# Fixed experts for the first eight pairs of tiles, early weights, and identity transposes where TensorE waits, in a six-stage decoder kernel

## The reference

```python
x = _layernorm(x + _L0_attn_ref(x, ...))      # 16 heads of 128, causal, rotary
x = _layernorm(x + _L0_xattn_ref(x, ctx, ...)) # 32 heads of 16, against the context
x = _layernorm(x + _L0_ffn_ref(x, ...))       # 32 routed experts (4 of them each token, capacity 80) and a shared one
x = _layernorm(x + _L1_attn_ref(x, ...))      # 16 heads of 32, along the other axis
x = _layernorm(x + _L1_xattn_ref(x, ctx, ...)) # 16 heads of 128, RMS norm on q and k
x = _layernorm(x + _L1_ffn_ref(x, ...))
return x
```

```python
router_logits = x_flat @ gate_w.T                    # 8 experts
top_w, sel = jax.lax.top_k(router_logits, TOPK)      # TOPK = 2
top_w = jax.nn.softmax(top_w, axis=-1)
tw = jnp.zeros((n, E), dtype=x.dtype).at[tok_ids, sel].add(top_w)
g = jnp.einsum('nd,efd->enf', x_flat, gate_proj)     # F_DIM = 352
u = jnp.einsum('nd,efd->enf', x_flat, up_proj)
h = jax.nn.silu(g) * u
eo = jnp.einsum('enf,edf->end', h, down_proj)
out = jnp.einsum('end,ne->nd', eo, tw)
```

## Time and profile before

| | us |
|---|---|
| median of 3 runs | 3399.54 (3391.4 to 3400.45) |
| the profiled execution | 3412.12 |
| its span, first to last instruction | 3410.3 |
| PE busy in it | 3095.0 (91%) |
| DVE busy | 2215.1 (65%) |
| POOL busy | 1565.7 (46%) |
| ACT busy | 1446.3 (42%) |
| mean granted clock of PE | 0.957 |

### The profile page before, as it was taken

One profiled execution on the slowest core, in us unless ns is written; L12 is line 12 of the kernel. 1 busy time (PEld: TensorE's weight loads), 2 busy tenths in 40 slices (PEclk: granted clock), 3 DMA queues, 4 the chain that ended last, 5 costly groups with the idle time before them and its releaser, 6 DMA issues. The chain is left out here.

```text
span 3410.3 us, 57006 instructions
## 1 busy us (share of the span) xinstructions
PE 3095.0 (91%) x20208; PEld 2562.7 (75%) x20208; DVE 2215.1 (65%) x3877; ACT 1446.3 (42%) x3497; POOL 1565.7 (46%) x1466
## 2 busy tenths in 40 slices
PE   7999999999969999888897999699999999969992
PEld 5887878878857777665575777488888888759991
DVE  5667566567645677649775777556667677745555
ACT  3343333333336666528743333244444444324441
POOL 4544343344422343335573222355555556545555
PEclk9999999999979999889998999799999999979996
DMA  4001016022310111049612112311101001146765
GB/s 176 16 12 59 0 36 237 0 79 104 116 73 22 48 38 58 17 164 350 216 42 91 41 41 61 118 41 35 36 12 48 11 24 41 45 177 235 245 229 160
DMA packets 133264, 303.09 MB, mean 89 GB/s; under 512 B 21152, under 2 KB 33184, under 8 KB 126832
## 3 DMA queue, kind: packets, MB, share of 16 engines
q1 hardware_dynamic: 115584, 274.61, 23.6%
q0 software_dynamic: 15360, 22.16, 2.1%
q10 hardware_dynamic: 2160, 4.21, 0.4%
HBM read 231.07 MB, written 98.04 MB: 97 GB/s over the span
## 5 line engine op out<-in xcount | busy, mean ns | idle before, releaser
L398 POOL TENSOR_TENSOR a_sq<-a_tq,a_sinq 128x256 f32<-128x256 f32 x128 | 150.5, 1195 | 356.9 <-DVE a_tq L476 355.6
L364 ACT COPY a_probT<-bank 128x512 f32<-128x512 f32 x64 | 37.5, 586 | 329.1 <-PE bank L715 329.1
L398 POOL TENSOR_TENSOR a_sk<-a_tk,a_sink 128x256 f32<-128x256 f32 x128 | 123.8, 987 | 90.0 <-DVE a_tk L476 90.0
L411 POOL TENSOR_TENSOR e_sk<-e_tk 128x512 f32<-128x512 f32 x64 | 66.5, 1039 | 204.2 <-DVE e_tk L503 204.2
L348 ACT ACTIVATE a_sm<-a_sm,a_nmax 128x128 f32<-128x128 f32 x256 | 99.8, 391 | 122.6 <-DVE a_nmax L572 122.6
L353 ACT ACTIVATE e_prob<-bank,e_nb,e_rq 128x128 f32<-128x128 f32 x256 | 113.7, 454 | 86.4 <-DVE e_nb L577 86.4
L1048 POOL TENSOR_TENSOR d_prob<-d_prob,d_nmax 128x1024 f32<-128x1024 f32 x32 | 63.9, 1998 | 182.2 <-DVE d_nmax L1147 182.2
L954 ACT ACTIVATE b_prob<-bank,b_nb 128x128 f32<-128x128 f32 x512 | 139.1, 386 | 13.5 <-DVE b_nb L1152 13.2
L2334 POOL TENSOR_TENSOR m_down_lo<-cw_down,m_down_hi 128x1024 fp32r<-128x1024 f32 x32 | 93.2, 2912 | 106.4 <-ACT m_down_hi L2296 106.4
L2570 POOL TENSOR_TENSOR n_wu_lo<-nw_wu,n_wu_hi 128x1408 fp32r<-128x1408 f32 x23 | 74.3, 3232 | 128.0 <-DVE n_wu_hi L2614 128.0
L498 DVE TENSOR_TENSOR a_kr<-a_kr,a_sk 128x512 f32<-128x512 f32 x64 | 66.5, 1038 | 88.9 <-POOL a_sk L398 88.9
(11 more groups left out here) (562 smaller groups left out, 11126.9 us busy)
## 6 DMA issues: line engine op xcount, KB each, us to landing
packed<-all_zero SPq DMA_DIRECT2D x32, 1024.0 KB, 7.0
cw_up<-in_c_wgu SPq DMA_DIRECT2D x32, 1024.0 KB, 9.1
cw_down<-in_c_wd SPq DMA_DIRECT2D x32, 512.0 KB, 9.3
nw_wg<-in_f_wg SPq DMA_DIRECT2D x23, 704.0 KB, 5.9
nw_wu<-in_f_wu SPq DMA_DIRECT2D x23, 704.0 KB
nw_wd<-in_f_wd SPq DMA_DIRECT2D x23, 512.0 KB, 7.5
nw_xe<-packed SPq DMA_DIRECT2D x46, 256.0 KB, 2.7
result<-n_ye SPq DMA_DIRECT2D x46, 256.0 KB, 2.0
```

The source lines that it names most:

```text
L364: nc.scalar.copy(probT[:], pP[:, :]).then_inc(act_pt, 1)
L398: step = nc.gpsimd.tensor_tensor(o, i, s, ALU.mult)
```

## The change

Two things. First, a helper `keep_busy` issues n transposes of the identity into a bank that nobody reads, with no semaphore. It is put into PE's stream before and after `turn_x(0)` at the start of a, b, m, d, e and n, in the last unit of a and e (30 before the wait for the probabilities, 24 before the last output), and ahead of the last outputs of b and d. Nine matmuls on zeros are put in the first block.

Second, stages r and n: the first eight of the 23 pairs of tiles are now always expert 0 to 7's own first pair, so their expert and tile are known when the program is built, and only the pairs beyond come from the tables. SP loads the weights of pair 0 at once, waits for the sends, then issues the tiles of pairs 0 and 1, then the weights of pair 1. Two of r's ten sends move into the last unit of e, ahead of POOL's drain. DVE gets twelve more small operations: each expert's first pair and the rest now lie apart.

```diff
+def keep_busy(nc, bank, tile, n):
+    for _ in range(n):
+        nc.tensor.transpose(bank[:, 0:P], tile[:, 0:P], tile[:, 0:P])
...
                 if router and last:
+                    for n in (2, 3):
+                        router.send(pool, (b - 5) // 2, n)
                     pool.drain()
...
                 if r is not None and not last:
                     route(r)
+                if last:
+                    keep_busy(nc, pQ, ident, 30)
                 pe.wait_ge(v_p, done(u))
...
+            keep_busy(nc, pO, ident, busy[0])
             turn_x(0)
+            keep_busy(nc, pO, ident, busy[1])
             pe.wait_ge(g_lo, done(0))
...
             probs_v(u, 1)
+            keep_busy(nc, pQ, ident, 24)
             output(G - 1, B - 1)
...
+            keep_busy(nc, pP, ident, busy[0])
             turn_x(0)
+            keep_busy(nc, pP, ident, busy[1])
             pe.wait_ge(w_lo["q"], 1)
...
             each_batch(pe, slot)
+            keep_busy(nc, pJ, ident, busy[2])
             for e in plan["pe"][0]:
...
+            keep_busy(nc, pJ, ident, busy[3])
             output(B - 1, (0, 3 * C), False)
...
         def _(sp):
-            sp.wait_ge(tabled, 2)
+            weights.load(sp, weights.number(sp, 0, 0), 0)
+            sp.wait_ge(router.sent, 16 * K * B)
             for w in range(2):
-                weights.load(sp, weights.number(sp, 0, w), w)
-                if w == 0:
-                    sp.wait_ge(router.sent, 16 * K * B)
                 weights.load_x(sp, ..., weights.place(sp, 0, w), w)
+            weights.load(sp, weights.number(sp, 0, 1), 1)
...
         def _(pool):
-            for n in (2, 3):
-                router.send(pool, LAST - 2, n)
...
+            step(vec.tensor_scalar(first[:], first[:], float(NE), None, ALU.add))
...
+            step(vec.tensor_scalar(tsum[:], tsum[:], float(1 - NE), 0.0, ALU.add, ALU.max))
...
+            for each_expert, out in ((edge, pos), (low, own), (more, over)):
+                step(vec.tensor_tensor(prod[:], hot[:], each_expert[:]..., ALU.mult))
+                step(vec.tensor_reduce(out[:].rearrange("p b k -> p k b"), prod[:], AX.X, ALU.add))
+            step(vec.tensor_tensor(pos[:], rowf[:], pos[:], ALU.is_ge))
+            step(vec.tensor_tensor(over[:], over[:], pos[:], ALU.mult))
+            step(vec.tensor_tensor(own[:], own[:], over[:], ALU.add))
+            step(vec.tensor_tensor(rows[:], rowf[:], own[:], ALU.add))
...
+            keep_busy(nc, pO[1], ident, 12)
             turn_x(0)
+            keep_busy(nc, pO[1], ident, 6)
...
     def number(self, sp, i, w):
+        if isinstance(i, int) and 2 * i + w < self.NE:
+            return 2 * i + w
         return sp.value_load(self.expert[0:1, bass.ds(2 * i + w, 1)], ...)
...
-            with sp.Fori(0, ROUNDS - 1) as i:
+            FIXED = weights.NE // 2 - 1
+            for i in range(FIXED):
+                for w in range(2):
+                    refill(i, w)
+            with sp.Fori(FIXED, ROUNDS - 1) as i:
...
             turn_x(0, 0)
+            keep_busy(nc, pO[1], ident, 10)
             in_turns(pe, slot, ROUNDS, R, REST)
...
+                for _ in range(9):
+                    nc.tensor.matmul(psum[7][:, 0:P], zero[:, 0:P], zero[:, 0:P], start=True, stop=True)
```

More of the change, by code:

```diff
@@ L83, in split_product, with wide_attention @@
     return nc.tensor.matmul(ps, a_hi, b_hi, start=False, stop=stop)
-def wide_attention(nc, name, psum, ident, x_src, x_dst, w_dram, staged, head, rope=None, rms=None, background=None, keep=None, ahead=None, head_ready=False, router=None):
+def wide_attention(nc, name, psum, ident, x_src, x_dst, w_dram, staged, head, rope=None, rms=None, background=None, keep=None, ahead=None, head_ready=False, router=None, busy=(0, 0)):
     G, H = 4, 4
@@ L739, in _, with narrow_attention @@
             probs_v(u, 1)
+            keep_busy(nc, pQ, ident, 24)
             output(G - 1, B - 1)
-def narrow_attention(nc, name, banks, ident, x_src, x_dst, w_dram, NH, plan, staged, head, rope=False, causal=False, keep=None, router=None, ahead=None, head_ready=False):
+def narrow_attention(nc, name, banks, ident, x_src, x_dst, w_dram, NH, plan, staged, head, rope=False, causal=False, keep=None, router=None, ahead=None, head_ready=False, busy=(0, 0, 0, 0)):
     DH = D // NH
@@ L2108, in end_of_routing @@
         pos, prod = st.sbuf("pos", [P, B, K]), st.sbuf("prod", [P, K, B, NE])
+        low, more, edge = st.sbuf("low", [P, NE]), st.sbuf("more", [P, NE]), st.sbuf("edge", [P, NE])
+        own, over = st.sbuf("own", [P, B, K]), st.sbuf("over", [P, B, K])
         apart, expd, total = st.sbuf("apart", [P, B]), st.sbuf("expd", [P, B]), st.sbuf("total", [P, B])
@@ L2114, in end_of_routing @@
         texp, tsum = st.sbuf("texp", [P, NP]), st.sbuf("tsum", [P, NP])
-        act_e, v_c, tabled = st.sems("act_e", "v_c", "tabled")
+        act_e, v_c = st.sems("act_e", "v_c")
         block = ctx.enter_context(nc.Block())
@@ L2148, in _ @@
             each = [P, NE, NE]
-            step(vec.tensor_scalar(limit[:], iota[:, 0:NE].unsqueeze(1).to_broadcast(each), float(PAIR), None, ALU.mult))
+            step(vec.tensor_scalar(limit[:], iota[:, 0:NE].unsqueeze(1).to_broadcast(each), float(PAIR), float(PAIR), ALU.mult, ALU.add))
             step(vec.tensor_tensor(limit[:], limit[:], region[:].unsqueeze(2).to_broadcast(each), ALU.add))
@@ L2167, in _ @@
             step(vec.tensor_reduce(texp[:], past[:], AX.X, ALU.add))
-            vec.tensor_scalar(weights.expert[:], texp[:], float(NE - 1), None, ALU.min).then_inc(tabled, 1)
+            step(vec.tensor_scalar(weights.expert[:], texp[:], float(NE - 1), None, ALU.min))
             step(vec.tensor_tensor(before[:], past[:], npair[:].unsqueeze(1).to_broadcast([P, NP, NE]), ALU.mult))
@@ L2171, in _ @@
             step(vec.tensor_tensor(tsum[:], iota[:, 0:NP], tsum[:], ALU.subtract))
+            step(vec.tensor_scalar(tsum[:], tsum[:], float(1 - NE), 0.0, ALU.add, ALU.max))
             step(vec.scalar_tensor_tensor(out=tsum[:], in0=texp[:], scalar=float(REGION // PAIR), in1=tsum[:], op0=ALU.mult, op1=ALU.add))
[L2173 to L2178, removed]
+            step(vec.tensor_scalar(weights.tile[:], tsum[:], 2.0, float(NE * REGION // P - 2), ALU.mult, ALU.min))
+            step(vec.tensor_scalar(edge[:], region[:], float(PAIR), None, ALU.add))
+            step(vec.scalar_tensor_tensor(out=low[:], in0=iota[:, 0:NE], scalar=float(PAIR), in1=region[:], op0=ALU.mult, op1=ALU.subtract))
+            step(vec.scalar_tensor_tensor(out=more[:], in0=first[:, 0:NE], scalar=float(PAIR), in1=edge[:], op0=ALU.mult, op1=ALU.subtract))
+            step(vec.tensor_tensor(more[:], more[:], low[:], ALU.subtract))
+            for each_expert, out in ((edge, pos), (low, own), (more, over)):
+                step(vec.tensor_tensor(prod[:], hot[:], each_expert[:].unsqueeze(1).unsqueeze(1).to_broadcast([P, K, B, NE]), ALU.mult))
+                step(vec.tensor_reduce(out[:].rearrange("p b k -> p k b"), prod[:], AX.X, ALU.add))
[3 more added lines that the diff above has]
+            step(vec.tensor_tensor(rows[:], rowf[:], own[:], ALU.add))
             dve.wait_ge(act_e, 1)
@@ L2437, in place @@
     def place(self, sp, i, w):
+        if isinstance(i, int) and 2 * i + w < self.NE:
+            return (2 * i + w) * (REGION // P)
         return sp.value_load(self.tile[0:1, bass.ds(2 * i + w, 1)], min_val=0, max_val=self.NE * REGION // P - 2)
@@ L3013, in _ @@
                 nc.gpsimd.memset(zero[:], 0.0).then_inc(g_z, 1)
+            @block.tensor
+            def _(pe):
+                pe.wait_ge(g_z, 1)
+                for _ in range(9):
+                    nc.tensor.matmul(psum[7][:, 0:P], zero[:, 0:P], zero[:, 0:P], start=True, stop=True)
         def zero_rows(sp, v):
@@ L3037, in decoder @@
         wide_attention(nc, "a", psum, ident, x, x1, of("a_"), staged_a, head_a, rope=True, background=zero_rows, ahead=fetch_b,
-                       head_ready=True)
+                       head_ready=True, busy=(0, 30))
         with ExitStack() as moe:
@@ L3044, in decoder @@
             narrow_attention(nc, "b", banks, ident, lambda b: x1[b], None, {**of("b_"), "ctxT": ctxT}, 32,
-                             PLAN_8, staged_b, head_b, rope=True, keep=xall, router=router, ahead=fetch_c, head_ready=True)
+                             PLAN_8, staged_b, head_b, rope=True, keep=xall, router=router, ahead=fetch_c, head_ready=True, busy=(20, 36, 0, 34))
             EARLY, QUADS, XE = 4, 3, 4
@@ L3060, in decoder @@
             combine_beside(nc, "cc", base, result1, router.rows, weight, zero, x2, 4, rest, staged_d.fetch)
-        narrow_attention(nc, "d", banks, ident, lambda b: steps[0][b], lambda b: steps[1][b], of("d_"), 16, PLAN_4, staged_d, head_d, causal=True, ahead=fetch_e)
```

(3 more changed lines are left out.)

## The result

The change is faster: 3379.31 us (5 runs, 3375.22 to 3381.44) against 3396.99 (5 runs, 3389.64 to 3400.45), a ratio of 0.9951, 95% interval 0.994 to 0.9961, or 13 to 20 us. Forecast were 15.4 us and 3384.

The account below looks back on a forecast made before the run. PE was taken to bound the kernel, busy in 91% of the span, with gaps at stage seams. Terms summed to 15.35 us; from the median 3399.5 less 15.4 that gave 3384 us, range 3366 to 3398 (own range 3375 to 3392).

Parts of the forecast that it names:

- a's end: End of stage a: 30 and 24 fillers fit their waits and the last two outputs run fast, +5.0 us, at least 2.7.
- b's last output: End of stage b: 34 fillers fit a wait of 4.38 us, output 3.0 for 4.93 us, +1.9 (-1 to 2.2).
- d's two: End of stage d: 42 and 30 fillers fit their waits, both outputs gain, +4.35 us (0 to 4.7).
- Starts: Starts of b and e: 20 fillers delay `turn_x(0)`, -2.1 us (0 to -2.6) and -2.9 us (-3.6 to 0).
- The start of d: 28 fillers in a wait of 4.80 us; first products gain if the clock is up, +0.8 us (0 to 0.8).
- that of m: Start of m: 12 fillers in a DMA wait of 4.57 us, no delay, faster transposes, +0.5 us (-0.5 to 1.6).
- End of e: 30 fillers net about -0.45 us, last output behind 24 fillers +1.65; together +1.2 us (-5.7 to 2.1).
- Stage r: Last send lands sooner, +4.6 us; no table reads in SP's queue, +2.0; DVE hidden by 3 us; +6.6 (2 to 8).
- B: Rival: fillers break even, delays at b's start and e's start and end eat the gains; only r pays: 3393, chance 0.17.
- D: Rival: the last scatter's 7.7 us are its own, not the weights' doing; r gives 2.0 for 6.6: 3388.8, chance 0.08.
- C: Rival: transposes don't count for the clock, fillers run at 0.21 us and outlast waits; slower, 3412, chance 0.07.
- E: Rival: clock stays up in slow stretches after the starts of b and d, 7 to 8 us more: 3376, chance 0.13.

Follow-up runs that it names:

- the second: The unchanged change timed again on the same chip as two variants, against the kernel before: 3383.84 us (6 runs), ratio 0.9967.
- that with a third: The change with a third of the fillers at each place (the 9 first matmuls stay): 3382.33 us, ratio 0.996 to the kernel before.
- no start: The change without the 20 fillers ahead of `turn_x(0)` in b and in e: 3374.85 us, ratio 0.9936 to the kernel before.
- trimmed: The change without fillers ahead of `turn_x(0)` in b and e, 16 for 36 behind it in b, 8 for 30 at e's end: 3374.3 us, ratio 0.9938.
- the fillers alone: The kernel before with all fillers at all their places and nothing else: 3386.58 us, ratio 0.9976 to the kernel before.
- the late weights: The change, but SP waits for both tables before loading pair 0's weights, as before: 3387.46 us, ratio 0.9977 to the kernel before.

## Why the prediction was right

**The sum.** Direction, size and range held: 16.6 us in the first comparison for 15.4 forecast; the second, 7 to 15 us, has it at its edge. The mechanisms held as well, but the closeness of the sum is partly luck: single terms were off by 1 to 3 us in both directions, as shown here.

**Ends of stages.** In the two profiles compared, a's end gave 19.4 - 14.4 = 5.0 us (forecast 5.0), b's last output 4.9 - 3.1 = 1.8 (1.9), d's two 5.1 - 3.0 and 5.2 - 3.0, 4.3 (4.35). Here the luck is plain: what I read was one execution, and over the three without fillers a's end averages 17.9, which makes the term 3.5. I carried the terms of the profiled execution over to the median at full size; that step was 1.5 us too good. With fillers a's end takes 14.4 in every profile but that with a third: they take out the chance.

**Starts.** Forecast -2.1 and -2.9. a>b grows from 16.3 to 18.1 on the average of three and six profiles, -1.8; d>e from 15.3 to 18.6, -3.3. At d>e the runs "no start" and "trimmed" show it to be those 20. But the gap is not the whole price. From a's last output product to b's first scores it is 31.1 to 32.1 us in the three profiles without fillers and 34.3 to 34.9 in the six with all of them, 3.0 us more; "no start" has 32.7, trimmed 31.3. Two of the rows in between, the first product with V's weights, in the changed kernel and before it:

```profile
994.85 0.80 PE L1263 MATMUL bank<-b_wv_hi,b_s_lo 128*128 128x512 f32 x1 [3.07 <-POOL b_wv_lo L1043]
998.58 0.50 PE L1250 MATMUL bank<-b_wv_hi,b_s_lo 128*128 128x512 f32 x1 [1.09 <-POOL b_wv_lo L1030]
```

The fillers made b's first 12 products fast (3.0 us for 4.7 to 5.2), but the next ones wait for POOL, which is 1.8 us late with everything behind `turn_x(0)`. So PE only waits longer, 3.07 us, and V's six products then come at clock 0.50, in 2.93 us. In the seven other profiles the wait is 0.8 to 1.7 us, and these products take 1.7 at clock 1.00. The term for the start of b was therefore too small: it took the slack of 1.63 us in front of the first product for the slack of the whole start. In e it is the other way round: from d's last output product to the 97th with e's weights, the six profiles take 66.7 us on average and the three without fillers 65.7, so of the 3.3 us some 2 come back, though the six scatter from 64.3 to 68.6. The start of d, +0.8 forecast, is worth 0.9; that of m can't be told from the scatter.

**End of e.** Forecast +1.2; the two profiles compared give 20.3 - 18.7 = 1.6, but the usual is 3.3 (20.3 to 17.0). The 30 mostly ran at the higher clock and cost less than the 3.6 to 4 that I took. This term was mis-sized by 2 us, on the safe side.

**Stage r.** Forecast 6.6, measured 7.2 in the two profiles compared (39.43 to 32.23). The landing gave 5.0 for 4.6: from the last send's issue to the end of SP's wait 7.7 us before and 2.7 now. SP's queue behind that wait took 5.9 us and takes 3.8, 2.0 as forecast. DVE's end stayed hidden by 2.2 us, not 3.

**The rivals.** B fell with the fillers alone, D with the late weights. C, that transposes leave the clock low, fell with every output behind a full row of them, and with the rise of the clock at the start of b behind nothing but fillers. The page of the Trainium skill that speaks for it, "TensorE: Matmul & The Clock Gate", Part 4, does not fit this kernel: after 30 and 24 f32 transposes the output took 3.0 us. E, warmth that lasts in b and d for 7 or 8 us, does not show: b takes 446.5 to 452.3 us without fillers and 446.4 to 450.1 with them, and its average is the same (449.0 and 449.2 in the three and six profiles), since the 1.8 us at its end are lost again at its start. Over d's first 96 products the gain is about 1 us, the 0.9 of its start. In e, of which E said nothing, the first 96 products take 49.1 to 51.2 us without fillers and 46.0 to 49.9 with all of them, 2 us less on average; whether that is warmth or chance stays open.

## What to carry to other kernels

Price a filler by what it stands ahead of: in a wait for another engine it is free up to the wait's length, ahead of the only instruction that is ready it costs its length, less what slack there is, and a trace shows which it is by the idle time left in brackets. Follow a delay at a start past the first product: slack in front of one product is not slack in front of the next, and a fast stretch ahead of a wait for another engine only makes the wait longer. Start a transfer whose address is known before the ones that somebody waits for, rather than beside them. And read terms that depend on the clock from more than one execution; the seams that don't depend on it repeat to some tenths, while the others differ by several us in one unchanged kernel.

## What was not expected of the hardware

Two executions of the unchanged kernel differed by 19.6 us of span, spread over a, b, b>m, m>d and n in pieces of 3 to 4 us; behind an equal wait of 2.92 us the clock was once low (last output 5.5 us) and once high (3.0). Behind a wait of 8.46 us the clock rose from 0.50 to 1.00 while PE ran f32 transposes alone. The last indirect scatter of 128 rows let its reader go 2.7 us after its issue when the last weights had been issued 12 us ahead of it, and 6.9 us after it with 1.9 MB of weights issued within 1.2 us of it; in the kernel before, with such weights beside it, SP's wait ended 7.7 us after it.
